# A Mamba scan on four engines: projection items ahead of the state sums, GpSimd's inflow products one slot later

## The reference, cut to what matters

```python
xi, z = split(x @ in_proj_w.T)                       # 512 channels each
xc = silu(conv_b + causal_conv4(xi))
dt, Bm, Cm = split(xc @ x_proj_w.T)                  # 16, 16, 16
dt = softplus(dt @ dt_proj_w.T + dt_proj_b)
def step(h, inp):                                    # per token
    h = exp(dt * A) * h + (dt * xc) * Bm             # 512 x 16 states
    return h, sum_n(h * Cm)
y = (ys + xc * D) * silu(z)
out = y @ out_proj_w.T
x = layernorm(x + layernorm(out_forward + flip(out_backward)))
```

## Time and profile before

| | us |
|---|---|
| median of 3 runs | 3083.71 (3078.88 to 3086.35) |
| profiled execution | 3078.34, its span 3076.5 |
| this stage, of the span | about 48 to 998 |
| busy over the whole span: PE / DVE / ACT / POOL | 2630.4 / 1914.4 / 1356.5 / 1140.8 |
| scans, line 498 | 256 of 2278 ns, idle before them 44.2 |
| products, line 196 | 256 of 2458 ns, idle before them 102.8 |
| state sums, line 264 | 1024 matmul records, busy 509.2, idle before them 92.6 |

### The profile page before, as it was taken

The page is one execution under the profiler, slowest core; times in us unless marked ns, Lnnn a source line. Parts: engine busy times, 40 slices in busy tenths (PEclk is TensorE's granted clock), DMA queues, the critical chain, the costliest instruction groups (busy, mean ns, idle before and its releaser), DMA issues. The chain is left out here.

```text
span 3076.5 us, 46270 instructions
## 1 busy us (share of the span) xinstructions
PE 2630.4 (86%) x18034; PEld 1511.2 (49%) x18034; DVE 1914.4 (62%) x3210; ACT 1356.5 (44%) x2378; POOL 1140.8 (37%) x595
## 2 busy tenths in 40 slices
PE   6988988988977679999975799997689998887698
PEld 2333433433423234545444676775445555666487
DVE  3899999999997287878784112222246676555323
ACT  4656556556552266676662111111155565132132
POOL 3888888888887033333331400003200000200030
PEclk8999999999999889999997799998899999898599
DMA  5022032032020723343331601111200000200020
GB/s 197 6 111 110 8 116 110 8 116 110 8 109 8 259 50 78 81 93 77 71 90 48 281 13 35 32 34 58 79 1 1 1 1 1 83 8 1 1 98 28
DMA packets 126983, 201.72 MB, mean 66 GB/s; under 512 B 8128, under 2 KB 101568, under 8 KB 114608
## 3 DMA queue, kind: packets, MB, share of 16 engines
q1 hardware_dynamic: 122432, 185.26, 18.6%
q0 software_dynamic: 4336, 13.50, 1.3%
HBM read 169.12 MB, written 29.62 MB: 65 GB/s over the span
## 5 line engine op out<-in xcount | busy, mean ns | idle before, releaser
L196 POOL TENSOR_TENSOR m_h<-m_h,m_bc 128x1024 f32<-128x1024 f32 x256 | 623.5, 2458 | 102.8 <-DVE m_h L498 102.5
L498 DVE TENSOR_TENSOR_SCAN m_h<-m_da,m_h 128x1024 f32<-128x1024 f32 x256 | 579.0, 2278 | 44.2 <-ACT m_da L394 43.6
L264 PE MATMUL m_psy<-m_h,m_ident 128*128 128x512 f32 x1024 | 509.2, 626 | 92.6 <-POOL m_h L196 92.6
L394 ACT ACTIVATE m_da<-m_dt,m_a_neg 128x511 f32<-128x511 f32 x512 | 330.7, 681 | 179.7 <-DVE m_h L498 171.3
L264 PEld LDWEIGHTS m_psy<-m_h,m_ident 128*128 128x128 f32 x1024 | 193.7, 196 | 370.3 <-issue 221.5
L898 POOL TENSOR_SCALAR c_pr<-c_pr,c_share 128x512 f32<-128x512 f32 x128 | 200.0, 1562 | 429.8 <-DVE c_share L1179 429.8
L485 DVE TENSOR_TENSOR m_h<-m_dtx,m_bc 128x1024 f32<-128x1024 f32 x192 | 231.8, 1208 | 1.8
L959 PEld LDWEIGHTS c_psO<-c_pT,c_vr 32*64 32x64 f32 x8192 | 129.8, 136 | 138.6 <-issue 135.4
L959 PE MATMUL c_psO<-c_pT,c_vr 32*64 32x128 f32 x8192 | 161.3, 287 | 37.5 <-ACT c_oT L1070 32.4
L1055 ACT ACTIVATE c_pr<-c_pr,c_nmx 128x512 f32<-128x512 f32 x256 | 180.8, 707 | 3.7 <-DVE c_nmx L1172 3.5
L1061 ACT ACTIVATE c_pr<-c_pr,c_share 128x512 f32<-128x512 f32 x128 | 92.3, 721 | 194.3 <-DVE c_share L1179 194.1
(11 more groups left out here) (324 smaller groups left out, 4429.4 us busy)
## 6 DMA issues: line engine op xcount, KB each, us to landing
m_bc<-bc_dram SPq DMA_DIRECT2D x32, 2048.0 KB, 7.4
c_vr<-v_dram SPq DMA_DIRECT2D x128, 256.0 KB
v_dram<-c_stage SPq DMA_DIRECT2D x32, 256.0 KB
e_up<-in_up SPq DMA_DIRECT2D x8, 1024.0 KB
e_down<-in_down SPq DMA_DIRECT2D x8, 1024.0 KB
xs_dram<-c_oT POOLq DMA_DIRECT2D x1, 4992.0 KB, 29.9
e_buf<-xs_dram SPq DMA_DIRECT2D x39, 128.0 KB
y_dram<-e_buf SPq DMA_DIRECT2D x39, 128.0 KB, 1.7
```

Source lines behind the costliest of these rows:

```text
L196: pool.tensor_tensor(hq, hq, bc[:, 1, NP * s:NP * (s + 1), :], ALU.mult).then_inc(p_ready, 1)
L264: mm = pe.matmul(bank, ident[:], h[:, n % HB, e, :], start=False, stop=(s == NG - 1 and e == NP - 1))
L394: ins = act.activation(da[:, n % 2, e, at:at + L - 1], dt[:, u, j, at:at + L - 1], ACT.Exp, scale=a_neg[:, u, j, NP * s + e:NP * s + e + 1])
L498: dve.tensor_tensor_scan(flat, decay, flat, 0.0, ALU.mult, ALU.add).then_inc(scanned, 1)
```

## The change

Three edits, all in `mamba_stage`:

```diff
@@ gpsimd
                     pool.wait_ge(scanned, n + 1)
                     pool.tensor_tensor(hq, hq, bc[:, 1, NP * s:NP * (s + 1), :], ALU.mult).then_inc(p_ready, 1)
-                    if n + 4 < NU * QN and (n + 4) % NG in POOL_AT:
-                        inflow(n + 4)
+                    if s == 4:
+                        inflow(n - s + POOL_AT[1])
+                    if s == 0 and n > 0:
+                        inflow(n + POOL_AT[0])
@@ tensor
                 for i in range(NU):
                     for q in range(QN):
-                        state_sum(i, q)
                         if i == 0 and q < NJ:
                             in_proj(0, NJ + q)
...
                         if i >= 1 and 12 <= q < 16:
                             out_proj(i - 1, (q - 12) // 2, q % 2)
+                        state_sum(i, q)
@@ vector
-                        if i >= 1 and i % 2 == 0 and q in (15, 17):
-                            add_out(i - 1, (q - 15) // 2)
+                        if i >= 1 and i % 2 == 0 and q in (16, 18):
+                            add_out(i - 1, (q - 16) // 2)
```

## The result

| | before | after |
|---|---|---|
| median, us | 3088.84 (3072.58 to 3101.06, 20 runs) | 3080.15 (3069.97 to 3091.59, 20 runs) |
| profiled execution, its span | 3076.5 | 3079.6 |
| first scan to last output sum | 943.4 | 934.7 |
| unit 0, scan to scan | 124.0 | 126.9 |
| units 1 to 6 together | 703.6 | 687.9 |

The ratio of the changed kernel to the one before is 0.9972, with a 95% interval of 0.9960 to 0.9984: 8.7 us faster by the medians, just under the 0.3% that the prediction called the same. The forecast was 12.0 us, which this interval (5 to 12 us) doesn't rule out. The time forecast, 3071.7 us, was 8.4 us too low: 5.1 us of that is that the kernel before ran 5.1 us slower over these 20 runs than in the three it started from. The measured time lies in the prediction's wide range, 3050 to 3092, and 2 us above the 3063 to 3078 of its main case.

What follows compares the result with a forecast made beforehand. VectorE paces the scan stage, idling for late ScalarE and TensorE. Gains of 41.5 us in units 1 to 6 and 2.1 in unit 0, less 31.6 of costs, net 12.0: from 3083.7 to 3071.7 us, range 3050 to 3092.

Steps and rivals of the forecast that it cites:

- wide range: Whole kernel: 3050 to 3092 us, leaving out the slower rival and the far end of the first.
- main case: Whole kernel: net 12.0 us faster, 3071.7 us, own range 3063 to 3078; chance 0.51.
- unit 7: Last unit: three dt·xc caught cost 3.2 us, a later last product in front of the last gate 1.0 us.
- GpSimd's part: Scan stage: product 5 ends later, so dt·xc takes 2.4 us; cost 18.0 us in units 1 to 6, softplus 8.4.
- TensorE's part: Items ahead of sums end 1.7 to 1.9 us earlier; of ScalarE waits, 28.9 us, 0.48 stays at each q=29.
- Output sums: Units 2, 4, 6: one slot later, the sums no longer wait for TensorE; 13.1 us go.
- Unit 0: First unit: wait at q=29 gains 2.1 us; third product and a held first sum cost 1 us; softplus 1.2 later.
- its third product, and a first sum held behind a second item: Unit 0: the third product and a first sum delayed behind a second item on TensorE, 1 us cost.
- The lock: First rival: VectorE gets in front of product 5, dt·xc takes 0.67 us; 3035 to 3060 us, chance 0.15.
- head start: Rival at q=0 to 7: bank handovers cost TensorE more than 1.9 us, ScalarE's waits stay; 3102 us, chance 0.12.
- if an inflow waits for a sum: Scan stage: one of two signs named as proving the prediction wrong; the other was scan 3 waiting for GpSimd's inflow.
- rival of the lower clock: Unit starts, holes at q=1 and q=26: a slow stretch costs TensorE 1.7 us, 10 us in all; 3082 us, chance 0.22.

Runs made afterwards that it cites:

- the run of GpSimd's move: GpSimd's reordering alone, on the kernel before: 941.3 us from first scan to last output sum, against 943.4 before.
- the sums first: Changed kernel with unit 0's first four state sums ahead of their items again: unit 0 124.4 us, first scan to last output sum 932.3.
- The held version: Changed kernel, GpSimd's product 5 waiting until VectorE's dt·xc is done: 3054.26 us, ratio 0.9879; first scan to last output sum 900.6, in the timed run's profile 906.9.

## Why the prediction was nearly right

**Sum.** Without the level of the kernel before, it is -12.0 forecast and -8.7 measured.

| | forecast | measured |
|---|---|---|
| units 1 to 6 | 41.5 gained, 18.0 + 7.2 paid: -16.3 | -15.8 |
| unit 0 | 2.1 gained, 1.0 + 1.2 paid: +0.1 | +2.9 |
| unit 7 | +4.2 | +4.2 |

**GpSimd's part.** Right in mechanism, place and size. Product 5 was to end 20.0 behind scan 0, and did (431.76 - 411.75). dt·xc was to have a median near 2.4, and has 2.42:

```profile
L480 DVE TENSOR_TENSOR m_dtx<-m_dt,m_xc x32: 701/2418/2880, 49.9 to 943.2; 128x512 f32<-128x512 f32 x32
```

Of the 18 counted in units 1 to 6 the sum is 43.5 against 42.3, as the third group took 2.57 to 2.88 in odd units. Softplus was to start 1.2 us later or last that much longer: it lasted 1.02 longer, 7.1 us in seven units instead of 8.4. Scan 3 didn't wait. At the end the last gate stood 6.25 us instead of 5.24, the 1.0 us of the forecast. VectorE, last unit:

```profile
978.80 0.69 DVE L506 TENSOR_TENSOR m_gz<-m_gz,m_psy 128x512 f32<-128x512 f32 x1 [6.25 <-PE m_psy L266]
```

**TensorE's part.** Right in the waits: 0.41 us left at q=29, where the forecast had 0.48, and none at q=14, 17 and 22. The price that I set at nothing in units 1 to 6 was nothing. The attribution was incomplete: I took the gain for TensorE's alone, and the run of GpSimd's move showed that it makes 19.1 us of the same gain when it stands alone. The sum didn't suffer, since both were made. The prediction did have GpSimd's part as a cost on top of TensorE's, and that is what the runs show: 15 to 16.5 us.

**Output sums.** The 13.1 us went, all of them.

**Unit 0** is the term that was mis-sized: +0.1 forecast, +2.9 measured. The prediction puts "its third product, and a first sum held behind a second item" at 1 us. The three dt·xc issued within the unit were all caught (2.72, 2.80 and 2.35 us instead of 0.67, 1.67 and 0.88): 4.7 us. Softplus took 1.0 more, as forecast, and VectorE's waits went from 14.7 to 11.7, 3.0 us where 2.1 was forecast: together +2.7 of the +2.9. I had seen the first sum held and stopped there. The next step was to follow it: the sum starts 15.7 us behind the first scan instead of 4.8, GpSimd's inflow 7 waits 5.50 us for the next one, product 5 comes late, and the first of the three dt·xc, free before, is caught. That one is 2.05 us. The second and third cost 2.6 us more, and still do with the sums first (2.79 and 2.38).

**The rivals.** The lock did not fall the other way: VectorE asked 0.5 us behind product 5 in most groups. It was closer than that in some, 0.34 us in the third group of unit 1 and 0.03 in that of unit 5, where this rival was near. TensorE's granted clock in units 1 to 6 was 0.97 against 0.96 before, so no loss there, though the 3082 us of that rival lies closer to the measured time than the forecast. The items did get their head start. The point at which I said I would be wrong, "if an inflow waits for a sum", came true, in unit 0 only.

**The chances.** I gave 0.54 to faster by over 0.3% and 0.34 to a smaller difference, which came. The expected 12.0 us was 2.7 us over that line, and one term that was 2.8 us too small took it just under.

## What to carry to other kernels

Two reorderings that free the same engine don't add: cost each of them alone, and then the second on top of the first, before making both. Where two engines exclude each other by order of arrival, write the order down with a semaphore so that the short instruction on the path goes first; here one wait on the engine with slack was worth 34 us of the stretch, where the whole change brought 8.7. And a change to a steady loop is to be walked through its first pass by itself, where twice the work stands in each slot.

## What the runs showed of the hardware

**A blocked instruction counts as busy.** VectorE's share in unit 5 rose from 109.56 to 114.31 of 115 us while it did the same work; a row whose median is far over its minimum (2.42 against 0.70 us for dt·xc) is where such time is found.

**The wait has a fixed end.** 288 of the dt·xc in ten of these profiles took over 0.8 us, 0.87 to 2.89; each of them ended 0.55 to 0.57 us behind the end of a GpSimd product that had begun before it.

**Both sides pay.** Softplus, 2.29 us alone, was 3.31 when a GpSimd product was ahead of it, and the GpSimd products of units 1 to 6 lost 20.4 us to VectorE.

**TensorE's clock is not the same in two executions of one program.** The held version has a hole of 3.3 us on TensorE at q=20 of unit 0, in front of a dt_proj item. The first execution's timeline and that of the timed one, at that hole and some 10 us later. First:

```profile
137.97 1.09 PE L244 MATMUL m_rot<-m_dbl,m_dt_w 16*128 16x512 f32 x2 [3.29 <-ACT m_dt L348]
...
148.23 3.70 PE L268 MATMUL m_psy<-m_h,m_ident 128*128 128x512 f32 x8
```

Second:

```profile
138.81 2.04 PE L244 MATMUL m_rot<-m_dbl,m_dt_w 16*128 16x512 f32 x2 [3.30 <-ACT m_dt L348]
...
152.21 5.47 PE L268 MATMUL m_psy<-m_h,m_ident 128*128 128x512 f32 x8
```

The windows from 138.9 to 154.2, in the same order:

```profile
138.90:154.20 15.30, 15.30 (x27) 5.56 (x27) 15.30 (x10) 10.74 (x17) 15.22 (x8) 0.78 0.00 0
```

```profile
138.90:154.20 15.30, 15.30 (x17) 4.68 (x18) 12.88 (x9) 7.99 (x12) 14.28 (x7) 0.50 0.00 1
```

In the second the granted clock is 0.50 (1.2 GHz) for the whole window, and in the first it is at 2.4 GHz for a good part of it. Behind the hole the scans of the second execution are 4.9 us later than those of the first, with a wait of 4.18 us of VectorE for a sum; another 1.4 us had come by the sixth scan of the unit: over the 16.6 us from the first scan the granted clock is 0.50 in the second and 0.59 in the first. Together they are the 6.3 us by which unit 0 is longer. The prediction's rival of the lower clock had the chain right (a slow stretch of TensorE comes back as waits of VectorE). It had the size too small, 1.7 us a stretch, and the place wrong: the clock struck in unit 0, in a version with little slack, and not in each unit of the changed kernel. How often it happens stays open: it was in one profile of the two.

**The rest of the program varies more than the change.** The part behind the last output sum took 2091.7 and 2082.4 us in the two profiles, and 2043 to 2099 in all of these profiles, with that code the same. Which of its stages varies was not followed up.
